# Two attention layers on one core: the transposed z by DMA instead of TensorE, the steps written out

## The reference

```python
xn = layernorm(x) * ln_w + ln_b
q = softmax(xn @ Wq + bq, within each head's features)
k = softmax(xn @ Wk + bk, over the tokens; masked tokens get -1e6 or -inf)
v = (xn @ Wv + bv) * mask
att = k^T v per head                 # features x features
y = q @ att per head
scale, shift = split(silu(emb) @ W_emb + b_emb)
h = layernorm(y) * (1 + scale) + shift
x = x + silu(h) @ W_out + b_out
```

## Time and profile before

| | before |
|---|---|
| median of 3 runs | 350.72 us |
| profiled execution, span | 348.4 us |
| PE busy | 324.6 us (93%) |
| DVE busy | 277.7 us (80%) |
| ACT busy | 263.6 us (76%) |
| POOL busy | 193.7 us (56%) |
| DMA, mean over the span | 52 GB/s |

### The profile page before, as it was taken

The page is one execution under the profiler, slowest core; times in us unless marked ns, Lnnn a source line. Parts: engine busy times, 40 slices in busy tenths (PEclk is TensorE's granted clock), DMA queues, the critical chain, the costliest instruction groups (busy, mean ns, idle before and its releaser), DMA issues.

```text
span 348.4 us, 8324 instructions
## 1 busy us (share of the span) xinstructions
PE 324.6 (93%) x2328; PEld 250.1 (72%) x2328; DVE 277.7 (80%) x903; ACT 263.6 (76%) x587; POOL 193.7 (56%) x460
## 2 busy tenths in 40 slices
PE   2689999999999999999999999999999999998844
PEld 2347777877777788778878778777788777776632
DVE  4455799888888888897889888889888888866742
ACT  4235767888777877777868888888898988877650
POOL 1252656666666666666464866666666666623160
PEclk9969999999999999999999999999999999999976
DMA  6699000000000001000000011111111111100001
GB/s 219 220 382 328 24 18 4 28 8 7 15 15 15 15 15 15 15 15 18 14 4 17 0 47 47 41 39 33 24 45 45 45 45 45 45 33 31 31 2 60
DMA packets 16567, 18.05 MB, mean 52 GB/s; under 512 B 1761, under 2 KB 14753, under 8 KB 16545
## 3 DMA queue, kind: packets, MB, share of 16 engines
q1 hardware_dynamic: 15280, 17.12, 15.3%
q10 hardware_dynamic: 1264, 0.66, 0.7%
HBM read 13.55 MB, written 4.23 MB: 51 GB/s over the span
## 4 chain that ended last, share of the span: by engine, by line
PE 86%; DVE 5%; DMA 3%; POOL 2%; issue 2%; ACT 1%; SPq 0%; POOLq 0%; DVEq 0%
PE ps_qv L1135 24%; PE ps_eo L1248 12%; PE ps_zk L1118 11%; PE ps_att L1193 9%; PE ps_y L1212 8%; PE ps_qy L1228 4%; PE ps_qv L1139 4%; PE ps_eo L1168 4%; PE ps_zk L1103 4%; PE ps_qy L1152 4%; DMA m1r<-in_mask_row 1%; DMA m_row<-mask_rows 1%; PE ps_y L1089 1%; PE ps_att L1089 1%; POOL x_plus L616 1%
## 5 line engine op out<-in xcount | busy, mean ns | idle before, releaser
L1135 PE MATMUL ps_qv<-w_hi,z_hi 128*128 128x512 f16 x128 | 49.3, 385 | 4.0 <-DVE bias_hi_lo L747 4.0
L547 POOL TENSOR_SCALAR y_ve<-y_mv 128x2 f32<-128x2 f32 x32 | 6.5, 202 | 81.6 <-DVE y_mv L910 81.6
L1135 PE MATMUL ps_qv<-w_lo,z_hi 128*128 128x512 f16 x128 | 49.3, 385 | 0.0
L1135 PE MATMUL ps_qv<-w_hi,z_lo 128*128 128x512 f16 x128 | 49.3, 385 | 0.0
L806 DVE SCALAR_TENSOR_TENSOR z_lo<-ps_zk,z_hi 128x512 f16<-128x512 f32 x32 | 22.0, 688 | 24.3 <-ACT z_hi L345 24.3
L616 POOL TENSOR_TENSOR x_plus<-x_all,row_b 128x512 f32<-128x512 f32 x32 | 40.7, 1271 | 0.6
L433 ACT ACTIVATE z<-x_all,x_shift,x_rstd 128x256 f32 (+1 forms) x64 | 34.5, 586 | 6.9 <-POOL x_shift L552 6.9
L1248 PE MATMUL ps_eo<-wo_hi,g_hi 128*128 128x256 f16 x128 | 36.0, 282 | 3.5 <-DVE x_all L931 1.7
L1212 PEld LDWEIGHTS ps_y<-att_e,eq_t 128*128 128x128 f32 x256 | 33.8, 190 | 6.1 <-issue 2.1
L1248 PE MATMUL ps_eo<-wo_hi,g_lo 128*128 128x256 f16 x128 | 36.1, 282 | 0.0
L1248 PE MATMUL ps_eo<-wo_lo,g_hi 128*128 128x256 f16 x128 | 36.1, 282 | 0.0
(11 more groups left out here) (100 smaller groups left out, 899.5 us busy)
## 6 DMA issues: line engine op xcount, KB each, us to landing
m_row<-mask_rows SPq DMA_DIRECT2D x32, 128.0 KB, 3.1
out<-x_all SPq DMA_DIRECT2D x16, 256.0 KB, 2.2
x_all<-in_x SPq DMA_DIRECT2D x1, 2560.0 KB, 13.2
wemb<-in_w_emb SPq DMA_DIRECT2D x2, 1024.0 KB, 9.2
w_raw<-in_w_in SPq DMA_DIRECT2D x2, 768.0 KB, 6.6
x_all<-in_x SPq DMA_DIRECT2D x1, 1024.0 KB, 6.5
row_b<-in_rows SPq DMA_DIRECT2D x2, 384.0 KB, 7.1
x_all<-in_x ACTq DMA_DIRECT2D x2, 256.0 KB, 4.4
```

The lines of the kernel that those rows point to most:

```text
L1135: last = mm(ps_qv[t][:, :], zz[p][:, c * S + t * P:c * S + (t + 1) * P], w[l][:, c * W + D:(c + 1) * W], start=(n == 0), stop=(n == 3 * C ...
```

## The change

- z is no longer transposed by PE. POOL makes z (`x_normalise`, two tensor_scalar) instead of ACT, right after `x_scale`. ACT's `z_high` and DVE's `z_low` read z from SBUF as tokens by features and write z_hi and z_lo in that layout. SP then issues two DMA transposes per item, z_hi to zt_hi and z_lo to zt_lo (128x512 float16 each); `project_k` waits for both, and `project_k` and `project_qv` read zt_hi and zt_lo, whose blocks stand in another order.
- `z_high` is now the first operation of ACT's step. `z_low` keeps its place in DVE's step, and waits also for the transposes of the item two before; in `finish` it comes earlier.
- The columns v_mask and ab_col, which POOL copied for every item, are gone; ACT reads item_col directly.
- All steps are written out; the loops, the register values and `wait_apart` are gone.
- The bulk loads that SP issued in steps 0 to 3 are issued by ACT, in the same steps (`later_loads`).

The diff, cut to its core:

```diff
         def steps(engine, run, finish=None):
-            for front in range(0, 6):
-                run(Step(0, front))
-            with engine.Fori(6, B - 1, 2) as r:
-                for u in range(2):
-                    run(Step(r, u, 0))
...
+            for front in range(LAST):
+                run(Step(front))
...
         # SP
             def step(s):
-                m, done = at(s, 0), at(s, 4)
+                m, tz, done = at(s, 0), at(s, 1), at(s, 4)
...
                     sp.dma_start(m_row[p][:, :], row.partition_broadcast(P)).then_inc(m_row_in[p], 16)
-                if s.static and s.front == 0:
-                    load_sequences(2, 4, x_in[2])
...
+                if tz.exists:
+                    j, p = tz.index, tz.parity
+                    sp.wait_ge(z_hi_ready, j + 1)
+                    if not tz.first_two:
+                        sp.wait_ge(qv_done[T - 1], j - 1)
+                    sp.dma_start_transpose(zt_hi[p][:, :].rearrange("p (m r) -> p m r", r=P), z_hi[p][:, :])\
+                      .then_inc(zt_in[p], 16)
+                    sp.wait_ge(z_lo_ready, j + 1)
+                    sp.dma_start_transpose(zt_lo[p][:, :].rearrange("p (m r) -> p m r", r=P), z_lo[p][:, :])\
+                      .then_inc(zt_in[p], 16)
                 if done.exists and done.layer == 1:
                     sp.wait_ge(x_new, done.index + 1)
...
         # ACT
             def z_high(a):
-                act.wait_ge(zt_done, j + 1)
-                if not a.first_two:
-                    act.wait_ge(qv_done[T - 1], j - 1)
-                nc.scalar.activation(z_hi[p][:, :], ps_zk[:, :], ACT.Copy, scale=Z_SCALE).then_inc(z_hi_ready, 1)
+                act.wait_ge(z_ready, j + 1)
+                if not a.first_two:
+                    act.wait_ge(zt_in[p], 16 * (j - p))
+                nc.scalar.activation(z_hi[p][:, :], z[p][:, :], ACT.Copy, scale=Z_SCALE).then_inc(z_hi_ready, 1)
...
             def step(s):
+                if tz.exists:
+                    z_high(tz)
                 if aa.exists:
                     exp_q_turned(aa)
...
-                if tz.exists:
-                    z_high(tz)
...
-                if f.exists:
-                    normalise(f)
+                later_loads(s.front)
...
         # POOL
+            def x_normalise(a):
+                j, p = a.index, a.parity
+                pool.wait_ge(x_shift_ready, j + 1)
+                if not a.first_two:
+                    pool.wait_ge(z_lo_ready, j - 1)
+                for t in range(T):
+                    last = pool.tensor_scalar(part(z[p], t), x_all[:, a.sequence * N + t * D:a.sequence * N + t * D + D],
+                                              x_rstd[p][:, t:t + 1], x_shift[p][:, t:t + 1], ALU.mult, ALU.add)
+                last.then_inc(z_ready, 1)
...
                 if f.exists:
                     x_scale(f)
+                    x_normalise(f)
                 if aa.exists:
                     add_out_bias(aa)
-                    ab_columns(aa)
-                if tz.exists:
-                    v_columns(tz)
...
         # DVE
                 dve.wait_ge(z_hi_ready, j + 1)
-                vec.scalar_tensor_tensor(z_lo[p][:, :], ps_zk[:, :], Z_SCALE, z_hi[p][:, :], ALU.mult, ALU.subtract)\
+                if not a.first_two:
+                    dve.wait_ge(zt_in[p], 16 * (j - p))
+                vec.scalar_tensor_tensor(z_lo[p][:, :], z[p][:, :], Z_SCALE, z_hi[p][:, :], ALU.mult, ALU.subtract)\
                    .then_inc(z_lo_ready, 1)
...
         # PE
-            def turn_z(a):
...
             def project_k(a):
-                pe.wait_ge(z_lo_ready, j + 1)
+                pe.wait_ge(zt_in[p], 16 * (j - p) + 32)
+                if not (a.index == 0):
+                    pe.wait_ge(k_neg_ready, j)
...
-                        for w, zz in ((w_hi, z_hi), (w_hi, z_lo), (w_lo, z_hi)):
-                            last = mm(part(ps_zk, d), w[l][:, c * W + d * P:c * W + (d + 1) * P], part(zz[p], c),
+                        for w, zz in ((w_hi, zt_hi), (w_hi, zt_lo), (w_lo, zt_hi)):
+                            last = mm(part(ps_k, d).rearrange("p (t s) -> p t s", t=T),
+                                      w[l][:, c * W + d * P:c * W + (d + 1) * P],
+                                      zz[p][:, :].rearrange("p (t c s) -> p t c s", t=T, c=C)[:, :, c, :],
                                       start=(n == 0), stop=(n == 3 * C - 1))
```

## The result

The change makes the kernel slower: 367.26 us (median of 4 runs, 365.29 to 371.99) against 350.57 us (350.33 to 350.96), a ratio of 1.046 with a 95% interval of 1.042 to 1.050. The forecast was 342.4.

A forecast was written before the change was run, and what follows sets the result against it. PE, 93% busy, was taken to bound the kernel, a latency ring only 0.17 us under its pace. Steady part -6.8, fill -1.0, finish -0.5 took the span from 348.4 to 340.1; plus 2.3 gave 342.4 us, range 333 to 361.

The forecast's parts named there:

- The second ring: Latency loop attend, DVE to y statistics, POOL to y_z, turn_y, attend: 9.11 us, limiting the saving on PE.
- POOL's new work at nothing: z on POOL adds about 0.3 us a step, covered by POOL's idle time before y_ve, so costs nothing.
- turn_z leaves PE: -0.43: Dropping one group of four PE transposes shortens PE's own work from 9.28 to 8.85 us a step.
- PE's ring: PE's own work, step after step, setting the pace before the change: 9.28 us in a written-out step.
- the film steps: Three steps with film products, expected to stay PE-bound and lose 0.43 us each: 29.8 instead of 31.1 us.
- The loops, -2.6: Writing the loops out removes 0.13 us of register work from each of 20 steps: 2.6 us.
- L: Time from the end of z_lo to PE's release by its DMA transpose: 2.7 us, ends 1.5 and 5.0.
- 6.04 + L: Step time if the transpose is late: 6.04 us from project_k to z_lo's end, plus L.
- The fill, -1 with -4 to +4: Start of the kernel: earlier project_k of item 1 gains 1.5 to 3.8 us, slower steps 3 to 5 lose up to 3.
- The late transpose: Rival: PE waits at project_k once L passes 3.1 us; 362.9 us with L = 4.0; chance 0.22.
- Serial blocks: Rival: a transpose's four blocks go one after another, L = 6 us, step 12 us, over 405 us; chance 0.08.
- PE alone at 8.85: Rival: PE alone sets the steady pace at 8.85 us a step, 335.5 us in all; chance 0.12.

The follow-up runs named there:

- e13: e8 with PE's turn_exp_k moved into the middle of the first qv product: 347.33 us, ratio 0.986 to the kernel before.
- e5: The changed kernel with POOL's k_add put ahead of x_plus: 361.45 us, ratio 1.032 to the kernel before.
- e3: All of the change but the DMA transposes, PE transposing z as before: 346.64 us, ratio 0.991 to the kernel before.
- e11: e1 with turn_z moved ahead of turn_exp_k on PE, nothing added or removed: 358.48 us, ratio 1.023 to the kernel before.
- e10: e5 with PE's turn_exp_k in the middle of the first qv product, ACT's order kept: 365.43 us, ratio 1.042 to the kernel before.
- e1: The kernel before with only its loops written out: 347.36 us, ratio 0.991 to the kernel before.
- e4: The changed kernel with SP issuing both transposes first, then the store, then the next m_row: 368.15 us, ratio 1.049 to the kernel before.
- e6: The changed kernel with the bulk loads back on SP, ahead of a step's transposes: 369.25 us, ratio 1.054 to the kernel before.
- e8: The change with PE transposing items 0 to 3, DMA the other 28, with e4's and e5's orders: 350.09 us, ratio 0.997 to the kernel before.
- e14: e13 with PE transposing the first six items instead of four: 345.21 us, ratio 0.985 to the kernel before.
- e2: The changed kernel with z made by ACT again instead of POOL: 363.16 us, ratio 1.033 to the kernel before.
- e9: e5 with turn_exp_k in the middle of the first qv product and ACT's ek_row copy ahead of y_z: 373.05 us, ratio 1.063 to the kernel before.

## Why the prediction was wrong, point by point

- **The second ring: the mechanism right, one link mis-sized.** e13 runs at 9.12 in layer 1. In the change itself the wait was where I put it, 0.36 us at turn_y. But the ring didn't stay as I had summed it. I took DVE's 5.08 us from att_e to y_mv as fixed, and it became 5.49: g_lo, one of its links, meets x_plus, and the step became 9.56 instead of 9.15 (e5 brings back 0.30 of it).
- **POOL's new work at nothing: the step that failed in the steady steps.** I costed POOL's time by who waits for its results, and wrote that nobody waits for x_plus within a microsecond. True, and the wrong question: DVE is held up while x_plus runs. It isn't z on POOL by itself (e3 has it, at 9.26) but the moment at which x_plus starts. The kernel before had the meeting already, in the very stretch that I called free of waits:

```profile
198.53 1.27 POOL L616 TENSOR_TENSOR x_plus<-x_all,row_b 128x512 f32<-128x512 f32 x1
...
199.52 0.84 DVE L917 SCALAR_TENSOR_TENSOR g<-th,h 128x512 f32<-128x512 f32 x1
199.75 0.65 POOL L592 COPY ab_col<-item_col 128x4 f32<-128x4 f32 x1
```

  g ends 0.56 us after x_plus and takes 0.84 us where it takes 0.68 alone; and ab_col, whose 0.650 us I read as a sign for a gain only, ends 0.04 us after g.
- **A third bound, not seen.** "turn_z leaves PE: -0.43" was priced by PE's ring and the y_z ring. The chain turn_exp_k, ek_row, attend was 1.31 us long in before, just as long as the three transposes from turn_exp_k to attend, so it had no slack at all. It holds the film steps, which I had at -0.43 each for being bound by PE, at exactly their old 31.1, and the clean step at 9.26, only 0.1 to 0.2 us above the second ring. e11 and the film steps of e10 show it.
- **The loops, -2.6: right** (-3.2 in e1).
- **L at 2.7 us: right for a quiet queue** (2.3 to landing in layer 0), wrong beside other DMAs: up to 4.4 in layer 1, behind the store and m_row, where five of 13 steps took 9.8 to 10.5. For four of these the sum 6.04 + L of the late transpose holds within 0.1 us. I had said that a late z_lo delays the store and m_row; it was they that delayed z_hi's transpose, and zt_lo behind it. e4's order is worth 1.6 to 1.8 us of layer 1.
- **The fill, -1 with -4 to +4: the step that failed most.** It was 17.5 us in the profiled execution, 13 to 14 in e4 and e6, and 11.3 in e5. I had the price, 5.0 and 8.8 us for a DMA beside the loads, and charged it to steps of which I thought that they could take it, at 11 us each. L was 6.4, 4.1 and 7.9 us for the first three items, not 2.7 to 5.0: the k product of item 1 came at 28.16 and not at 21.2 to 23.5, and step 3 took 18.5 us (16.2 in e5). In the fill items follow one another through z_lo, the transpose and project_k, so L counts in full for item after item; and in some executions PE's clock, which I hadn't in the sum at all, then fell to the lower level: the same 32 film products take 6.64 us instead of 3.48. e8 gives 8.4 us of the fill back by 4 items.
- **The rivals.** The late transpose was the right mechanism in the wrong place: not in 23 steady steps, but in the fill and beside the stores. Serial blocks are refuted: 4 blocks of 128x128 land in 2.3 us, where the estimate from the Trainium skill ("VectorE: DVE Perf Modes", the three transpose paths) was 5.2; the other rule quoted ("Advanced Engine Details and Errata", X-Bar Transpose), as fast as regular DMAs, agrees roughly: 2.3 us for 128 KB, beside 2.2 for the 256 KB store and 3.1 for the 128 KB m_row. PE alone at 8.85 did not occur as a pace.

The fill also differs from execution to execution: e8's fill is 3.4 us longer than e3's, though PE transposes in both, and e13's, with e8's orders on SP and POOL, is only 1 us longer. In e8's trace the load of m1r took 5.53 us and the first m_row 5.41, in e13's 4.55 and 3.87, which is 2.5 us ahead of any DMA transpose; the orders don't make it. The swing of the steps in e10, e13 and e14 is open.

## What to carry to other kernels

Before a piece of work is taken off the busiest engine, look at what else runs in its time: if a copy on another engine begins before it and is needed after it, the piece is cover, and its removal is worth nothing until that copy moves. Moving the piece a place earlier, as in e11, measures this cheaply: if that costs its full length, there was no slack. Price an operation also by whom it holds up while it runs, and not only by who waits for its result. And a DMA that comes into a chain has to be priced where its neighbours are worst, in the fill and beside stores, and issued ahead of whatever isn't urgent; where the loads are still under way the old path is better (e8, e14).

## What the runs showed of the hardware

- A DMA transpose of 128x512 float16 from SBUF to SBUF takes 1.19 us of SP's queue and lands 2.3 us after its issue when little else moves; 2.7 to 7.9 us in the fill, beside bulk loads (e5 and the change), and about 4.2 behind a 256 KB store and a 128 KB row. The transposes raised the packets of the kernel from 16567 to 51399, those under 512 B from 1761 to 36576.
- A DVE operation with two sources in SBUF (g, g_lo) and POOL's x_plus don't run together. g_lo and g, 0.63 to 0.69 us alone, took 1.14 to 1.18 us in the clean steps of layer 0 of the change and e2, up to 1.74 elsewhere, and ended 0.54 to 0.57 us after x_plus, wherever in it they started. Where DVE started first (e5), x_plus grew from 1.27 to 1.70 and more. Which starts first decides who pays.
- PE's granted clock fell to 0.50, its 1.2 GHz level, in the fill of the change, of e2, e4 and e9, and 32 matmuls took 6.64 us instead of 3.48; in e5 and e10, whose PE waited there too, it didn't fall at these matmuls.
- A loop step whose indices and semaphore targets are in registers took 9.41 us, the same step written out 9.26.
